# VectorE's routing pieces moved to the ends of steps 8 to 11, and everything that hangs on the sending step moved by one

## What is computed

```python
xn = _layernorm(x, axis=-1)
s = _L0_attn_ref(xn, qkv_w, proj_w, proj_b)      # local attention, 32 heads of 8
g = _silu(_L0_ffn_ref(xn, router_w, ...))        # one expert of 8 for each token
x = x + s * g

# in _L0_ffn_ref:
logits = x @ router_w
expert_idx = jnp.argmax(logits, axis=-1)
score = jax.nn.sigmoid(jnp.max(logits, axis=-1))
xs = x * score[:, None]
for e in range(n_experts):
    m = (expert_idx == e)[:, None]
    xe = jnp.where(m, xs, 0.0)
    h = jax.nn.silu(xe @ gate_w[e]) * (xe @ up_w[e])
    out = out + jnp.where(m, h @ down_w[e], 0.0)
shared = jax.nn.silu(x @ shared_gate_w) * (x @ shared_up_w) @ shared_down_w
```

## Time and profile before

| | us |
|---|---|
| median of 3 runs | 595.69 (592.25, 595.69, 595.95) |
| the profiled execution, its own time | 597.03 |
| its span in the profile | 595.0 |
| PE busy | 545.0 (92%) |
| DVE busy | 440.0 (74%) |
| POOL busy | 253.8 (43%) |
| ACT busy | 240.7 (40%) |

### The profile page before, as it was taken

The page is one execution under the profiler, slowest core; times in us unless marked ns, Lnnn a source line. Parts: engine busy times, 40 slices in busy tenths (PEclk is TensorE's granted clock), DMA queues, the critical chain, the costliest instruction groups (busy, mean ns, idle before and its releaser), DMA issues.

```text
span 595.0 us, 10334 instructions
## 1 busy us (share of the span) xinstructions
PE 545.0 (92%) x3302; PEld 472.2 (79%) x3302; DVE 440.0 (74%) x1030; ACT 240.7 (40%) x506; POOL 253.8 (43%) x187
## 2 busy tenths in 40 slices
PE   1989999979998999999999999999999999989773
PEld 1747789858876899988899988899888878876662
DVE  6776867898758566566656656655899999989993
ACT  1464454526553433433443442353434454343210
POOL 7122333128885322322422422222466876966442
PEclk9979999989998999999999999999999999999987
DMA  8624533215634667767566757644233755646423
GB/s 304 210 80 141 190 121 124 90 53 181 193 107 138 198 191 208 209 192 211 158 183 212 213 169 213 203 134 133 62 59 59 99 79 83 89 60 92 60 36 54
DMA packets 106618, 83.17 MB, mean 140 GB/s; under 512 B 42181, under 2 KB 104773, under 8 KB 106437
## 3 DMA queue, kind: packets, MB, share of 16 engines
q1 hardware_dynamic: 90724, 65.07, 37.5%
q0 software_dynamic: 10224, 12.33, 12.5%
q10 hardware_dynamic: 5616, 5.11, 2.5%
HBM read 59.41 MB, written 27.00 MB: 145 GB/s over the span
## 4 chain that ended last, share of the span: by engine, by line
PE 60%; DVE 15%; POOL 8%; issue 5%; ACT 5%; DMA 4%; SPq 1%; ACTq 0%; DVEq 0%
PE psM L1002 11%; PE psV L952 11%; PE psS L927 8%; PE psM L1011 5%; PE psM L979 5%; PE psM L938 4%; PE psM L974 4%; PE psM L902 4%; POOL xnT L453 3%; DMA xnT<-ys_dram,slot 3%; PE psM L907 3%; POOL Sx L443 3%; DVE O L769 3%; PE psM L960 3%; DVE PTs L749 2%
## 5 line engine op out<-in xcount | busy, mean ns | idle before, releaser
L443 POOL TENSOR_TENSOR Sx<-Sx,mx 128x752 f32<-128x752 f32 x64 | 98.8, 1544 | 124.4 <-DVE mx L727 124.1
L952 PE MATMUL psV<-VB,PTs 128*128 128x132 f32 x1024 | 132.3, 281 | 16.5 <-DVE O L769 16.5
L952 PEld LDWEIGHTS psV<-VB,PTs 128*128 128x128 f32 x1024 | 126.2, 191 | 21.4 <-issue 20.0
L437 POOL TENSOR_TENSOR Sx<-Sx,cst 128x752 f32<-128x752 f32 x28 | 47.0, 1677 | 184.1 <-DVE Sx L717 184.1
L927 PE MATMUL psS<-kBD,qBD 128*128 128x188 f32 x512 | 97.8, 323 | 0.2 <-DVE Sx L717 0.2
L927 PEld LDWEIGHTS psS<-kBD,qBD 128*128 128x128 f32 x512 | 84.7, 190 | 9.5 <-issue 2.5
L749 DVE STREAM_TRANSPOSE PTs<-Sx 128x512 f32<-128x512 f32 x128 | 82.9, 685 | 4.2 <-ACT Sx L506 4.1
L717 DVE TENSOR_TENSOR Sx<-psS,cst 128x752 f32<-128x752 f32 x64 | 60.0, 938 | 30.0 <-PE psS L927 29.7
L769 DVE TENSOR_TENSOR O<-psV,rs 32x128 f32<-32x128 f32 x256 | 73.5, 287 | 4.8
L1002 PE MATMUL psM<-xT,EB 128*128 128x128 f32 x624 | 76.5, 276 | 0.2 <-DMA EB<-in_L_ffn_up_w 0.2
L1002 PEld LDWEIGHTS psM<-xT,EB 128*128 128x128 f32 x624 | 73.8, 192 | 2.5 <-ACT qBD L495 1.3
(11 more groups left out here) (107 smaller groups left out, 686.6 us busy)
## 6 DMA issues: line engine op xcount, KB each, us to landing
EB<-in_L_ffn_gate_w SPq DMA_DIRECT2D x39, 256.0 KB, 3.0
EB<-in_L_ffn_up_w SPq DMA_DIRECT2D x39, 256.0 KB, 3.7
EB<-in_L_ffn_down_w SPq DMA_DIRECT2D x39, 256.0 KB, 3.1
VB<-v_dram SPq DMA_DIRECT2D x256, 32.0 KB
stage<-xs_dram SPq DMA_DIRECT2D x39, 128.0 KB, 2.2
ys_dram<-yb ACTq DMA_DIRECT2D x39, 128.0 KB, 3.2
xs_dram<-blank SPq DMA_DIRECT2D x9, 512.0 KB, 3.2
v_dram<-vS SPq DMA_DIRECT2D x8, 512.0 KB, 3.0
```

The source lines that it names most:

```text
L443: nc.gpsimd.tensor_tensor(s, s, mx[n % 3][:, :].unsqueeze(2).broadcast_to([P, 2 * G, KW]), ALU.subtract).then_inc(a_sub, 1)
L952: last = mm(psV[:, j, at:at + HS * VW], PTs[n % 2][:, k, j, i, :], VB[n % 2][:, i, k, :, VW * j:VW * j + VW], start=k == 0, stop=k == 1)
```

## The change

The pieces of routing leave their place between `largest` and `flipped` and go to the end of DVE's step, behind `attention` and `choose`. They are spread differently: `rank` in step 8, `score` and `tiles_of` in step 9, `slots` in step 10, `table` in step 11. SENT becomes 11. Through it the sending runs in steps 11 to 17, E0 becomes 19, C_STEP 41, and the steps with a late mask and those of `silu` and `result` (but for the last two chunks) move by one. All other work stays in its step: attention, the shared expert, the projection and `attention(4)` in step 12.

```diff
-SENT = ROUTE + 2
+SENT = ROUTE + 3
...
-                if n == ROUTE:
-                    rank()
-                    tiles_of()
-                if n == ROUTE + 1:
-                    score()
-                    slots()
-                if n == ROUTE + 2:
-                    table()
                 if 0 <= n - 1 < U:
                     flipped(n - 1)
...
                 if n == ROUTE - 1:
                     choose()
+                if n == ROUTE:
+                    rank()
+                if n == ROUTE + 1:
+                    score()
+                    tiles_of()
+                if n == ROUTE + 2:
+                    slots()
+                if n == ROUTE + 3:
+                    table()
```

## The result

The changed kernel takes 605.45 us (median of 6 runs, 603.01 to 606.06), the kernel before 594.05 (6 runs beside it). The ratio is 1.0195, 95% interval 1.0171 to 1.0218: 2% slower, outside the range I gave. The profiled execution took 603.01 with a span of 601.2, which is the lowest of the six, 2.4 under their median; the one before took 597.03 with 595.0, which is 3.0 over the median of its runs. So the two traces stand 6 us apart where the medians stand 11.4 apart.

A forecast was written before the change was run, and what follows sets the result against it. PE bounds the experts, POOL's chain of sends the part from step 10 to them, PE and DVE nearly full last. Terms -0.2 before the experts and +0.2 in the last part sum to 0: 595.8 us, forecast 594.3 to 597.2, range 592.0 to 599.8.

The forecast's parts named there:

- The walk ahead of the experts: PE and DVE from 111.5 to the first expert matmul, step by step with POOL's sends: -0.2 us in sum.
- Attention(4) waits 4.8: Step 12: DVE reaches attention(4) at 146.4 and waits 4.8 us for scatter 7, landed at 151.2.
- PE idles 2.2 and 2.05 behind it: After attention(4): PE waits 2.2 us for weigh(13) and 2.05 us for division 11.
- First expert matmul at 198.9: Start of the experts on PE: 198.9 if step 18's hole halves the clock, against 191.31 before.
- So the gain is handed back in step 12: Step 12: PE, 3.7 us ahead in step 11, loses it to a wait that did not exist before.
- third rival: Idles of 2.2 and 2.05 in step 14 may halve PE's clock; where no cover is left +1.5, 597.3 us; chance 0.08.
- the last part: After the experts: silu(3) behind DVE's last wait +0.6, shorter silu waits 0.4 less; +0.2 us, bounds -0.4 and +1.2.
- The sign that I had named: Last part: waits of DVE for PE behind step 46 would show the forecast wrong.
- last waits for PE at 463.88: Last part, step 46: DVE's last wait for PE is at 463.88, and DVE is the bound from there.
- Rival 1: Step 12: the wait for scatters is longer and delays POOL's chain; slower, +3 us, 598.8; chance 0.17.
- Rival 4: Nothing that counts moves and only the last part shows: +1.2 us, 597.0; chance 0.08.
- the tail over 601.6: Whole kernel: more than 1% slower, from something not seen; chance 0.05.

The follow-up runs named there:

- E0: Not a run: a constant of the kernel's code, set as SENT + 8; the experts run from step 19 in the changed kernel. No time of its own.
- the pieces at the ends of steps 8 to 10: Kernel before with only its routing pieces moved to the ends of DVE's steps 8 to 10, SENT = 10, five scatters a step: 594.33 us, ratio 0.9994.
- the first experiment: Changed kernel with only the steps of silu and result set anew, so no silu stands in a step that is a multiple of 4: 595.39 us, ratio 1.0013.
- the version with shorter groups: Changed kernel with four scatters a step from step 10, a semaphore per group, routing pieces ending steps 8 to 10, silu and result reset: 589.68 us, ratio 0.9912.
- the kernel with the pieces at the ends and SENT = 10: Changed kernel with SENT back at 10, pieces at the ends of steps 8 to 11, E0, late masks, silu and result as before: 597.13 us, ratio 1.0052.

## Why the prediction was right and wrong

**The walk ahead of the experts held in the main.** The forecast has to be read 1.4 us earlier, by the lead in step 8. Slots with L697 at 0.42: so it was. Table at 1.4: 1.34. Attention(4) waits 4.8: 5.13. PE idles 2.2 and 2.05 behind it: 2.29 and 1.24, the second shorter. The last scatter at 187.3, so 185.9: 185.78. First expert matmul at 198.9, so 197.5: 197.33. "So the gain is handed back in step 12": yes, and most of it to POOL's chain if not there, as the pieces at the ends of steps 8 to 10 show. Two more sizes were off without harm: rank took 1.92 us for 2.35 (its scans no longer ran beside a subtraction), and PE waited 0.48 us for weigh(17), for 1.7. The granted clock fell to its lower level in step 14, behind the idle 2.29 us (L953 took 3.86 us for 2.00), which was the third rival's. It cost little: in the first experiment the clock stayed at 1.00 behind an idle time of 2.43, and its first expert matmul came 0.3 us earlier, counted from step 8.

**The step that failed is the last part.** I priced it +0.2 with bounds of -0.4 and +1.2; it cost 10 us (605.45 against 595.39 without it; 604.63 in the kernel before with it alone). "silu and result come one step later, while attention ends at step 63 as before" was true, and I looked at it on DVE alone: how much of its work moves behind its last wait for PE. The same sentence moves the tanh on ACT, ahead of the copies of the queries in four steps, and I put that at nothing without a reason. I asked of POOL what the moved sends would stand behind and did not ask it of ACT. What was needed stood ahead of the prediction: `silu_at` leaves out every fourth step, `jobs_of` puts the queries into every fourth, and ACT's loop has the one ahead of the other. The 1.33 us wait in the earlier trace rows is for that tanh; that ACT in its turn waited for a gather, I did not follow. The bounds were set for the mechanism that I had in mind, so they could not hold one that I had not. The sign that I had named for a failure in the last part, waits of DVE for PE behind step 46, did not show it either: none comes between 461.49 and 588.35 in the changed kernel. And "last waits for PE at 463.88" holds only up to step 63; in the last steps before, DVE waits for PE three times more (0.77, 1.34 and 1.42 us from 578 on).

**The rivals.** Rival 1 (a longer wait in step 12) gave slower, but not by this; the scatter landed as before. Rival 4 named the place, the last part, with a tenth of the size. None of them had ACT's queue. The result lies in the tail over 601.6, to which I had given 0.05.

**The sum without that step**, a change of 0, agrees with the first experiment's +0.7 us, though an interval of 0.25% (1.5 us) to either side cannot tell it from other small sums.

## What to carry to other kernels

Moving a constant that other schedules hang on moves all of them against those that stay; before a price is put on it, list for every engine what now meets in one step (here every fourth). An engine with 40% of busy time can hold two full ones, when an instruction that waits for a transfer stands ahead of copies that free a buffer: put the waiting one last in its step, or in a step that has no such copies. And an idle time that is seen is worth its length only if no other chain is as long as the bound engine's. Here one of sends, at 7.7 us a step, was, and taking the hole out alone gave nothing (594.33 for 594.81); the version with shorter groups was the only one that came out faster.

## What the runs showed of the hardware

A VectorE instruction can last until POOL's beside it ends. L697 took 1.55 us beside a subtraction of POOL and 0.42 without; the eight scans of L682 took 1.52 us beside one (POOL, 111.61 to 113.06) and 1.10 without; L707 took 0.80 us in the kernel before, where a subtraction ended at 132.46, and 0.18 in the changed one. Not every one does: the copies L678 and L679 out of PSUM took 0.42 and 0.41 us, beside the same subtraction as the scans or not. In the kernel with the pieces at the ends and SENT = 10 it was another instruction's turn (DVE's timeline; POOL's subtraction there runs from 140.54 to 142.00):

```profile
139.93 2.12 DVE L708 CAST etabi<-etabs 128x39 int32<-128x39 f32 x1
```

L708 took 0.18 us in the kernel before and in the changed one, and here it ended with the subtraction, at 142.05. The Trainium skill, SBUF — State Buffer, "Who interferes with whom", has a VectorE instruction with two SBUF inputs contend with a GpSimd instruction that reads SBUF; it has casts and `tensor_scalar`, where they run in two-port mode, contend with GpSimd too, and there whichever issues first blocks the other for a whole instruction. The ends of L697, L707 and L708 fit that. The start of L708 does not: by the trace it began 0.61 us ahead of the subtraction, beside a scatter of POOL (139.54 to 140.51), and in which mode it ran no row shows.

The same section of the Trainium skill has GpSimd kept from writing the descriptors of its DMAs while such a VectorE instruction runs. In the changed kernel table ran beside POOL's scatters; none of its four instructions was long (1.34 us in all), and the scatters beside it took 1.01 and 0.97 us as the second and third did before. So here that meeting cost nothing that the trace shows.
